# Linear attention on one core: the matrix queue as a loop over pairs of chunks, and the keys' feature map on GpSimd

## The reference, cut to what matters

```python
Q = _phi((x @ Wq).reshape(b, t, H, DH)).transpose(0, 2, 1, 3)   # _phi(x) = elu(x) + 1
K = _phi((x @ Wk).reshape(b, t, H, DH)).transpose(0, 2, 1, 3)
V = (x @ Wv).reshape(b, t, H, DV).transpose(0, 2, 1, 3)
S = jnp.cumsum(jnp.einsum('bhti,bhtj->bhtij', K, V), axis=2)
z = jnp.cumsum(K, axis=2)
num = jnp.einsum('bhti,bhtij->bhtj', Q, S)
den = jnp.maximum(jnp.einsum('bhti,bhti->bht', Q, z), EPS_DEN)[..., None]
return (num / den).transpose(0, 2, 1, 3).reshape(b, t, H * DV) @ Wo   # H = 16, DH = DV = 64
```

## Time and profile before

| | |
|---|---|
| device time, median of 3 runs (lowest, highest) | 854.55 us (852.06, 859.12) |
| profiled execution: time; span from first to last instruction | 862.1; 860.4 us |
| busy: PE, PEld | 93%, 78% |
| busy: DVE, ACT, POOL | 66%, 65%, 42% |
| transfers, mean | 40 GB/s |
| PE's code queue q8 | 93 packets, 1.52 MB |
| attention on PE | from about 201 to 629 us of the span |
| mean granted clock of PE | 0.992 |

### The profile page before, as it was taken

The page is one execution under the profiler, slowest core; times in us unless marked ns, Lnnn a source line. Parts: engine busy times, 40 slices in busy tenths (PEclk is TensorE's granted clock), DMA queues, the critical chain, the costliest instruction groups (busy, mean ns, idle before and its releaser), DMA issues.

```text
span 860.4 us, 26994 instructions
## 1 busy us (share of the span) xinstructions
PE 796.8 (93%) x11458; PEld 674.6 (78%) x11458; DVE 569.7 (66%) x1290; ACT 563.4 (65%) x1024; POOL 364.4 (42%) x292
## 2 busy tenths in 40 slices
PE   1799999998999999999999999999998799999997
PEld 0688888877788888888888788888786678888886
DVE  7665565376867787687787876778798582818220
ACT  3687777767565654646556556565677477777774
POOL 4597979682001001010000101001276497979784
PEclk9999999999999999999999999999999899999999
DMA  7002120201001001010010100201024320201010
GB/s 256 0 26 60 39 66 8 84 3 51 15 3 41 14 3 53 3 42 14 3 52 4 51 3 27 64 3 40 28 65 118 89 61 13 62 12 50 1 50 26
DMA packets 56762, 34.55 MB, mean 40 GB/s; under 512 B 1984, under 2 KB 55232, under 8 KB 56640
## 3 DMA queue, kind: packets, MB, share of 16 engines
q1 hardware_dynamic: 56640, 32.79, 13.2%
HBM read 22.29 MB, written 10.49 MB: 38 GB/s over the span
## 4 chain that ended last, share of the span: by engine, by line
PE 81%; ACT 6%; issue 5%; DVE 4%; POOL 2%; DMA 1%; SPq 0%; DVEq 0%; ACTq 0%; POOLq 0%
PE ps L677 34%; PE ps L822 21%; PE ps L648 9%; PE ps L886 4%; PE ps L913 4%; PE ps L869 4%; PE ps L898 4%; PE ps L740 3%; ACT ee L1158 1%; DVE xnA L1285 1%; ACT junk L1085 1%; ACT full L1123 1%; DMA xlnA<-x_scratch 1%; ACT gate L1047 1%; POOL alA L1662 1%
## 5 line engine op out<-in xcount | busy, mean ns | idle before, releaser
L1766 POOL TENSOR_TENSOR as<-as,power 128x4 f32<-128x4 f32 x16 | 16.7, 1045 | 292.6 <-DVE as L1485 247.9
L1158 ACT ACTIVATE ee<-ps 128x512 f32<-128x512 f32 x128 | 77.8, 608 | 95.5 <-PE ps L822 69.6
L1662 POOL TENSOR_TENSOR alA<-full,ahA 128x512 fp32r<-128x512 f32 x74 | 100.5, 1371 | 41.9 <-DVE ahA L1325 35.7
L1317 DVE SCALAR_TENSOR_TENSOR full<-ps,sc,gate 128x512 f32<-128x512 f32 x64 | 46.6, 747 | 104.2 <-PE ps L677 63.9
L677 PE MATMUL ps<-ahA,wh 128*128 128x512 f32 x288 | 113.5, 394 | 1.0 <-POOL alA L1662 1.0
L677 PE MATMUL ps<-ahB,wh 128*128 128x512 f32 x288 | 113.4, 394 | 0.1
L677 PE MATMUL ps<-alA,wh 128*128 128x512 f32 x288 | 112.2, 390 | 0.0
L677 PE MATMUL ps<-alB,wh 128*128 128x512 f32 x288 | 112.2, 390 | 0.0
L1662 POOL TENSOR_TENSOR alB<-full,ahB 128x512 fp32r<-128x512 f32 x76 | 99.1, 1318 | 13.0 <-ACT ahB L1066 7.3
L1065 ACT ACTIVATE full<-ps,sc 128x512 f32<-128x512 f32 x86 | 59.5, 692 | 33.3 <-PE ps L677 23.2
L1159 ACT ACTIVATE rr<-ps 128x512 f32<-128x512 f32 x128 | 78.0, 609 | 0.0
(11 more groups left out here) (179 smaller groups left out, 2248.1 us busy)
## 6 DMA issues: line engine op xcount, KB each, us to landing
wst<-in_ternary SPq DMA_DIRECT2D x5, 512.0 KB, 8.1
stage<-in_attn SPq DMA_DIRECT2D x4, 512.0 KB, 4.6
xlnA<-x_scratch SPq DMA_DIRECT2D x8, 256.0 KB, 2.8
axr<-x_scratch SPq DMA_DIRECT2D x8, 256.0 KB, 4.2
yx_scratch<-ay SPq DMA_DIRECT2D x8, 256.0 KB, 2.3
xs_scratch<-axs SPq DMA_DIRECT2D x8, 256.0 KB, 3.3
xlnA<-yx_scratch SPq DMA_DIRECT2D x8, 256.0 KB, 2.9
xlnB<-yx_scratch SPq DMA_DIRECT2D x8, 256.0 KB, 3.3
```

Source lines behind the costliest of these rows:

```text
L1158: nc.scalar.activation(ee[k][:, :], src[:, :], ACT.Exp).then_inc(*X["act"].step(f"e_{name}"))
L1317: nc.vector.scalar_tensor_tensor(fulll[m][:, :], ps[f["bank"]["L1", U, m, "v", n]][:, :], sc[:, KT + m:KT + m + 1], gate[k % NS][:, :], AL ...
L1662: return nc.gpsimd.tensor_tensor(dst, src, hi.bitcast(F32), ALU.subtract)
```

## The change

PE no longer runs through 32 written-out turns. It runs one pair of chunks written out, then a loop in the sequencer over 14 pairs with one body, then a last pair (`pair`, `last_pair`, `pe.Fori(1, NHALF - 1)`). Inside the loop the counts that waits need depend on the iteration, so each is worked out in a register (`hold`). To make all bodies alike: the state is no longer dropped between sequences but set to zero (the products with the zero state are made too), one buffer takes the place of two for the normalised half (`ahh`, `ahl`) and for the queries (`qf`), all four query tiles of a half are made in the second chunk of a pair, and WO of a half is made in the next pair, between V and KT. The keys' feature map goes from DVE to GpSimd, as a minimum and an addition. Unused buffers keep the other addresses as they were.

The core of the diff:

```diff
+            def hold(sem, value, per):
+
+                if rolled:
+                    value = pe.to_reg(rolled[0] * per + (value - per))
+                    if small:
+
+                        pe.wait_ge(X["pe"].sem, X["pe"].base)
+                pe.wait_ge(sem, value)
...
             def transposed_keys(n):
-                after("dve", f"phi_K{n}.1")
+                after("pool", f"phi_K{n}.1")
...
-                        for half, tok in halves if old else halves[1:]:
+                        for half, tok in halves:
...
-                both = n % CB < CB - 1
+                both = n + 1 < NC
...
+            def pair(hh):
+                e, o = 2 * hh, 2 * hh + 1
+                for h in range(2):
+                    token_major("K", o, h)
+                outputs(e)
+                norm(hh + 1)
+                for h in range(2):
+                    token_major("V", o, h)
+                if hh:
+                    output_projection(hh - 1)
+                transposed_keys(o)
+                if hh:
+                    back(hh - 1)
+                transposed_outputs(e)
+                state_products(o)
+                scores(o)
+
+                for h in range(2):
+                    token_major("K", o + 1, h)
+                outputs(o)
+                queries(hh + 1, 0)
+                queries(hh + 1, 1)
+                token_major("V", o + 1, 0)
+                queries(hh + 1, 2)
+                token_major("V", o + 1, 1)
+                queries(hh + 1, 3)
+                transposed_keys(o + 1)
+                transposed_outputs(o)
+                state_products(o + 1)
+                scores(o + 1)
...
+                pair(0)
+
+                with pe.Fori(1, NHALF - 1) as i:
+                    rolled.append(i)
+                    pair(1)
+                    rolled.pop()
+                X["pe"].next += (NHALF - 3) * X["pair"]["pe"]
+                last_pair(NHALF - 1)
...
                 if X["phis"].prior(name):
-                    after("dve", f"phi_{X['phis'].prior(name)[0]}")
+                    used = X["phis"].prior(name)[0]
+                    after("pool" if used[0] == "K" else "dve", f"phi_{used}")
...
+            def phi(n, h):
+
+                if n >= 2 and h == 0:
+                    after("pe", f"D{n - 2}.1")
+                k = X["phis"].place[f"K{n}.{h}"]
+                after("act", f"r_K{n}.{h}")
+                nc.gpsimd.tensor_scalar(ee[k][:, :], ee[k][:, :], 1.0, None, ALU.min).then_inc(*X["pool"].step(f"cap_K{n}.{h}"))
+                after("pool", f"cap_K{n}.{h}")
+                dst = kt_[n % 2][:, :].rearrange("p (k m d) -> p m k d", m=2, d=DH)[:, h, :, :]
+                e_, r_ = (a[:, :].rearrange("p (k d) -> p k d", d=DH) for a in (ee[k], rr[k]))
+                nc.gpsimd.tensor_tensor(dst, e_, r_, ALU.add).then_inc(*X["pool"].step(f"phi_K{n}.{h}"))
...
+            def attention_pool():
+                for h in range(2):
+                    phi(0, h)
+                root(1, "r1", "ve", ar1, av)
+                for hh in range(NHALF):
+                    c, i, e, o = 2 * (hh % 2), hh // 2, 2 * hh, 2 * hh + 1
+                    for h in range(2):
+                        phi(o, h)
+                    if c == 0 and i:
+                        residual(i - 1)
+                    if hh + 1 == NHALF:
+                        break
+                    phi(o + 1, 0)
+                    if c == 0 and i + 1 < NT:
+                        root(i + 1, "r2", "v3", ar2, av3)
+                    phi(o + 1, 1)
+                    if c == 2 and i + 2 < NT:
+                        root(i + 2, "r1", "ve", ar1, av)
```

More of the change, by code:

```diff
@@ L387, in kt, with outputs @@
                     act.append(f"kf{n}.{j}")
[L389 to L439, removed]
+            def outputs(g):
                 pe.extend(f"I{g}.{j}" for j in range(2))
@@ L496, in attention_plan @@
             X["banks"] = Banks([(j, b, e if type(e) is Made else X[e], by) for j, b, e, by in jobs], False)
+            X["pair"] = {e: pairs[2][e] - pairs[1][e] for e in ENG}
+            assert all(pairs[k + 1][e] - pairs[k][e] == X["pair"][e] for e in ENG for k in range(1, NHALF - 1))
             return X
@@ L789, in ffn_pe @@
                     if t == 2:
[L790 removed]
+                        back(NHALF - 1)
                     f_first(t, range(KT))
@@ L826, in norm @@
             def norm(hh):
-                after("dve", f"xn{hh // 2}")
-                transposes(bank(f"nT{hh}"), [axn[:, q, :] for q in (2 * (hh % 2), 2 * (hh % 2) + 1)], X["pe"], f"nT{hh}")
+                hold(*T["dve_ah"].done("xn", hh), 1)
+                transposes(bank(f"nT{hh}"), [axn[:, q, :] for q in range(2)], X["pe"], f"nT{hh}")
             def token_major(kind, n, h):
-                half, own = (n // 2) % 2, slice(h * DH, h * DH + P)
-                lh, ll = ahh[half][:, n % 2, own], ahl[half][:, n % 2, own]
+                own = slice(h * DH, h * DH + P)
+                lh, ll = ahh[:, n % 2, own], ahl[:, n % 2, own]
                 first = {"K": 1, "V": 2}[kind] * DA + h * TILE
                 cols = slice(first, first + TILE)
+                if kind == "K" and h == 0 and n % 2 == 0:
+                    after("dve", f"hl{n // 2}")
                 three(bank(f"{kind}{n}.{h}")[:, :], [(lh, ll, wah[:, cols], wal[:, cols])], f"{kind}{n}.{h}")
             def queries(hh, j):
-                after("dve", f"hl{hh}")
                 b = bank(f"Q{hh}.{j}")
@@ new lines, in attention_dve @@
+                        f_normalise(2)
+                        f_split(0, ("hi2", "lo3"))
+                        for j in range(2):
+                            low_outputs(o, j)
+                        f_stats(3)
+                        continue
+                    for j in range(2):
+                        divided(o, j)
+                    for j in range(4):
+                        phi(f"Q{hh + 1}.{j}")
+                    if hh + 2 < NHALF:
+                        twice(hh + 2)
+                    else:
@@ L1740, in ffn_pool @@
                 for t in range(2):
-                    f_rstd(t)
-                for t in range(2):
                     f_norm(t)
```

546 lines of the change are left out of this document (291 added, 255 removed).

## The result

The change made the kernel slower: 935.8 us (median of 4 runs, 935.2 to 942.6) against 854.9 us, a ratio of **1.096** [1.092, 1.101]. (The 854.9 has one execution more than the 854.55 of the table before.) The forecast was 868. The measured time lies in the range, 849 to 940, and close to the 932 us of the rival that fetches its code again, and both by luck: that rival's mechanism did not happen, and the forecast, whose mechanism did happen, had a range of its own that ended at 882. The one traced execution of the kernel before, 862.1 us, was longer than most of its others, so differences of a few us are taken from the medians, and one execution of a later version, of 3740 us, is left out of that version's ratio.

What follows compares the result with a forecast made beforehand. PE, nearly without a gap in the attention, was taken as the bound, at 26.1 us a pair. A pair of 26.8 gave +0.7 x 14 = 10, with 3.8 once +14: 854.55 + 14 = 868 us, range 849 to 940.

Steps and rivals of the forecast that it cites:

- the rival that fetches its code again: At the loop's branch back, each iteration fetches its code again: 3.62 us per branch, 932 us in all; chance 0.33.
- the powers among the keys: On GpSimd, r2 between key tiles adds 1.05 us in even pairs; r1 ahead of the next pair's keys adds 1.0.
- The minimum on GpSimd: In the key tile, the minimum takes 0.8 us, between a copy's 0.61 and the two-input form's 1.28; tile 2.1 us.
- The slow clock: PE's lower clock behind a long stall costs 1.7 us; counted at each branch back for code fetched again.
- the 3.8 us for the zero state: In I and D, 224 additional products with a zero state at 17 ns: +3.8 us once.
- The mean of 26.3: Mean length of a pair in the loop, from 27.3 us for even and 25.2 for odd pairs, before registers.
- PE's own sections, 24.5 us: PE's work in one pair without waits: 12.5 us for the first chunk, 12.05 for the second, together 24.5.
- Registers, +0.5 a pair: In each loop body, 45 more PE sequencer instructions; half of some 20 between small products are exposed: +0.5 us.
- Blocks that were read stay ... about 0.1 us: At the loop's branch, code is kept: branch back about 0.1 us, no fetches or code stalls from the second iteration.
- It was not what PE waited for, so I give no gain: DVE has 2.8 us a pair less to do without the key tiles, but no gain is counted.
- moving WO changes none of this: In PE's sections, moving WO leaves the 24.5 us a pair unchanged and only removes the wait for `ol` behind S.
- Short tile: On GpSimd, a minimum of 0.61 us makes the key tile 1.9 us; 858 us, or 851 with registers hidden; chance 0.25.

Runs made afterwards that it cites:

- The version whose waits are gone: Keys back on DVE in the changed kernel, registers worked out ahead, queries 0 and 1 between I and O, their DVE map ahead of the division: 853.1 us, 0.998.
- the last experiment: Changed kernel with queries and registers moved ahead, keys on GpSimd in the two-operation form, four buffers, powers behind the key tiles: 856.5 us, ratio 1.002.
- the price run: Changed kernel with keys back on DVE, plus nine operations on unused tiles by the otherwise idle GpSimd in each pair: 875.0 us, single execution.

## Why the prediction was wrong, step by step

**The forecast moved by +14 and the kernel by +81.** The mechanism was the right one: keys late from GpSimd, the ring of two buffers, the powers among the keys. Two terms were mis-sized, and one was put at nothing.

*The minimum on GpSimd, "I take 0.8".* It took 1.49. The bound "from above the two-input form, 1.28" was no bound: I had assumed that one input can't cost more than two, and no row says so. My sum with the right size: a tile is 1.49 + 1.29 + 0.07 = 2.85 us. In the second chunk K.1 is then read at 7.6 instead of 6.15, and D is late by 2.2 us; measured in the pair without powers, 1.77 ahead of query 3 and 0.33 ahead of the transposes, 2.1. Behind r1 the keys end at 10.9 against KT at 8.4, +2.5; measured 2.4. Ahead of query 3 in a pair with powers the sum gives 2.2 + 1.05 = 3.2; measured 2.6. So the arithmetic stands within some 0.6 us, and the price of one instruction was wrong.

*The slow clock.* I had priced it for the rival (1.7 us behind a stall), read from the earlier trace rows, but had left it out of my own waits, which were thought to be 1 us. With waits of 2.4 and 2.6 us it came: 3.4 us in four of the six pairs with powers. With the measured waits, 0.6 for registers and this, such a pair is 24.5 + 0.6 + 2.4 + 2.6 + 3.4 = 33.5 (measured 33.8), one without powers 24.5 + 0.6 + 2.1 = 27.2 (27.8).

*Outside the pairs, nothing but the 3.8 us for the zero state.* The spans show 9 us ahead of the loop, 5 in the last pair and 3 behind. With the keys on DVE the loop begins at 234.7 instead of 247.8 us, so GpSimd's keys cost 13 us ahead of it, 4.5 of them in one wait for tiles behind a power, a place that I had priced only inside the pairs. I had also put the 7.5 us between the traced execution and the median outside the pairs, without a reason; the one trace can't tell where they lie.

*The mean of 26.3.* It takes every second pair as one with powers, but I had named 6 or 7 of 16. By that count it is 26.0 to 26.1, and the forecast some 3 us lower; it changes nothing in the verdict.

*PE's own sections, 24.5 us.* Right. The loop's first chunk took 12.66 us where 12.5 were summed, registers included:

```profile
308.34:321.00 12.66, 12.66 (x313) 11.39 (x313) 7.66 (x19) 6.57 (x13) 5.52 (x4) 1.00 0.00 0
```

*Registers, +0.5 a pair.* Near. The version whose waits are gone has 25.1 us with part of the registers hidden; with 24.5 for the sections, 0.6 are left for registers and all else, and pairs without a stall are some 0.7 us longer with the loop than written out.

*"Blocks that were read stay ... about 0.1 us".* Right, with 0.21 for the branch. Its gain was smaller than the stalls it removed: 7 us with the keys on DVE, and none with the keys on GpSimd.

*"It was not what PE waited for, so I give no gain"* (DVE relieved): right, as the last experiment shows.

*The new order, "moving WO changes none of this".* Wrong by a little. Four queries in one chunk leave ACT behind at the transposes of the outputs: they took 1.54 us with the keys on DVE (412.07 to 413.61), and 1.15 when queries 0 and 1 had been moved ahead, 0.4 us a pair. With the zero-state products (3.8 us as summed, not tested) and 3 us in the stretch behind the attention this makes some 12 us, about the 11 (ratio 1.014) by which the written-out version with keys on DVE (867.6) lies above the kernel before. The parts were not tested one by one.

**The rivals.** Blocks fetched again: ruled out by 31 packets and 0.21 us; its 932 us fitted by chance, and 0.33 for it was too much of the range's upper end. Short tile: the opposite happened, and yet GpSimd *can* be that short, in a form I did not know of. With it the time is 883.6, not 858; four buffers and the new places of the powers, the queries and the registers together took away the other 27 us.

**The chances.** Slower had 0.65, which was the right side. The range's upper part came from the wrong case. With 1.5 us as the upper bound of the unknown price, the same sum gives 24.5 + 0.5 + 2.2 and, in every second pair, 1.05 + 2.5 more, a mean of 29.0: some 900 us, and some 925 with the slow clock of 3.4 us, as measured afterwards, in every second pair. That should have been the upper end of the forecast's own range.

## What to carry to other kernels

A price that no row shows has no upper bound in a row of another form: before work is moved to another engine, that one instruction is to be measured, in all the ways it can be written. A ring of two buffers hands the slower reader's lateness to everybody who shares it, here 45 us with a key tile of 2.85 us; count the reader of each place, not only the consumer of the result. And where PE waits some 2 us, put the slow clock that can follow (up to 1.7 us behind one wait here) into the sum, for one's own waits as for the rival's.

## What the runs showed of the hardware

- On GpSimd an operation with a number on 128x512 fp32 took 1.48 to 1.50 us with one operation and 0.62 with two (minimum, then maximum). Why is not settled; nine forms were measured in one execution, and this is the only one with two operations. Both lengths came again in whole kernels: 1.49 in the changed one, 0.62 in its two-operation version.
- PE keeps at least 5.1 blocks of 256 instructions: a loop body of 1,312 ran 14 times on one fetch. The taken branch took 0.21 us. I had given this only 0.42 and 0.25.
- Waits of equal length were not followed by the same clock: behind 1.77 us before 330.4 the clock was 0.75 for 6.8 us, and behind another 1.77 us, up to 451.8, it stayed at 1.00 over the whole pair. What tells the two apart stays open. Nor did the longest waits always bring it: the first pair with powers kept 1.00.
- GpSimd's times spread upwards: products of two tiles took 1.27 to 1.75 us in the price run, where DVE worked beside it much of the time, and the key's sum once 1.51 instead of 1.29, while DVE wrote a query tile (327.38 us). That DVE's work is the cause is not shown.
